# Convolution taps and the masked B C product read from PSUM, with a new order of the mixer step

## What is computed

```python
xn = rmsnorm(modulated layernorm of x)
z, xBC, dt = split(xn @ in_proj_w.T)                 # 1024, 1280 (1024 x + 128 B + 128 C), 16
pad = jnp.pad(xBC, ((0, 0), (DC - 1, 0), (0, 0)))    # DC = 4 taps, causal
conv = sum(pad[:, k:k + l, :] * conv_w[:, k] for k in range(DC)) + conv_b
xBC = conv * sigmoid(conv)
dt = softplus(dt + dt_bias)
# per chunk of 128 tokens, 16 heads of 64:
Y_diag = einsum('bcln,bcsn,bhcls,bcshp->bclhp', Cm, Bm, Lmat, X)   # (C B^T) masked, times exp(segment sums)
Y_off  = einsum('bcln,bchpn,bhcl->bclhp', Cm, states, exp(Acs))
y = (Y_diag + Y_off + D * xh) * (z * sigmoid(z))
y = rmsnorm(y); x1 = x + y @ out_proj_w.T
# then: layernorm, router (top 8 of 64 experts), experts, weighted sum
```

## Time and profile before

| | |
|---|---|
| median of 3 runs | 6409.54 us |
| the profiled execution | 6412.97 us |
| its span | 6411.1 us |
| PE busy over the span | 5781.9 us (90%) |
| DVE busy | 3957.1 us (62%) |
| ACT busy | 2733.7 us (43%) |
| POOL busy | 3763.9 us (59%) |
| mean granted PE clock | 0.951 |

### The profile page before, as it was taken

The page is one execution under the profiler, slowest core; times in us unless marked ns, Lnnn a source line. Parts: engine busy times, 40 slices in busy tenths (PEclk is TensorE's granted clock), DMA queues, the critical chain, the costliest instruction groups (busy, mean ns, idle before and its releaser), DMA issues. The chain is left out here.

```text
span 6411.1 us, 109995 instructions
## 1 busy us (share of the span) xinstructions
PE 5781.9 (90%) x28797; PEld 4345.1 (68%) x28798; DVE 3957.1 (62%) x10033; ACT 2733.7 (43%) x5780; POOL 3763.9 (59%) x2980
## 2 busy tenths in 40 slices
PE   2888888888888888888859999999999999999899
PEld 0556555565565565565548888888788888888787
DVE  1888888888888888888834444444344444444355
ACT  1555555555555555555513333333333333333322
POOL 0466666666666666666645555555555555555477
PEclk8899999999999999999979999999999999999999
DMA  9243343333343333333348887887877777887687
GB/s 351 107 124 119 106 131 120 111 130 107 117 136 105 119 125 105 122 122 105 129 123 194 196 217 173 213 196 175 228 155 176 186 164 179 211 214 196 106 269 256
DMA packets 338146, 1028.39 MB, mean 160 GB/s; under 512 B 55060, under 2 KB 59412, under 8 KB 337124
## 3 DMA queue, kind: packets, MB, share of 16 engines
q1 hardware_dynamic: 175512, 669.44, 30.3%
q0 software_dynamic: 145568, 321.56, 25.7%
q10 hardware_dynamic: 16816, 34.37, 1.4%
HBM read 580.45 MB, written 444.74 MB: 160 GB/s over the span
## 5 line engine op out<-in xcount | busy, mean ns | idle before, releaser
L1324 POOL DMA_INDIRECT acc_dram<-y_e,ids x576 | 907.9, 1576 | 1115.6 <-ACT y_e L1397 680.3
L1205 PE MATMUL bank<-w_hi,x_hi 128*128 (+1 forms) x2560 | 1058.0, 413 | 0.0
L1205 PE MATMUL bank<-w_hi,x_lo 128*128 (+1 forms) x2560 | 1002.3, 392 | 0.0
L1205 PE MATMUL bank<-w_lo,x_hi 128*128 (+1 forms) x2560 | 1001.5, 391 | 0.0
L938 DVE SCALAR_TENSOR_TENSOR acc<-raw,conv_w,acc 128x128 f32<-128x128 f32 x1920 | 820.3, 498 | 7.3 <-ACT acc L665 7.3
L602 POOL DMA_INDIRECT list_dram<-tok_id,pos x512 | 633.3, 1237 | 155.9 <-issue 154.6
L1415 DVE TENSOR_TENSOR h_lo<-bank,h_hi 128x256 fp32r<-128x256 f32 x576 | 243.5, 423 | 753.5 <-ACT h_hi L1386 746.8
L1397 ACT ACTIVATE y_e<-bank,xg_e 128x512 f32<-128x512 f32 x576 | 396.4, 688 | 693.4 <-PE bank L1205 649.1
L1316 POOL DMA_INDIRECT xg_e<-h_dram,ids x576 | 572.0, 993 | 195.0 <-issue 174.1
L1391 ACT ACTIVATE th_f<-bank 128x256 f32<-128x256 f32 x576 | 221.3, 384 | 1017.6 <-PE bank L1205 964.1
L770 PE MATMUL bank<-xn_t,w_in 128*128 128x128 f32 x5120 | 590.5, 277 | 66.4 <-ACT xn_t L644 66.4
(11 more groups left out here) (248 smaller groups left out, 10997.2 us busy)
## 6 DMA issues: line engine op xcount, KB each, us to landing
hi_dram<-w_hi_m SPq DMA_DIRECT2D x130, 768.0 KB, 7.4
lo_dram<-w_raw SPq DMA_DIRECT2D x130, 768.0 KB, 8.8
w_hi<-hi_dram SPq DMA_DIRECT2D x130, 768.0 KB
w_lo<-lo_dram SPq DMA_DIRECT2D x130, 768.0 KB
w_raw<-in_w_experts_dram SPq DMA_DIRECT2D x128, 768.0 KB
acc_dram<-zeros ACTq DMA_DIRECT2D x2, 16640.0 KB, 102.5
acc_c<-acc_dram SPq DMA_DIRECT2D x128, 256.0 KB, 3.5
h_dram<-h SPq DMA_DIRECT2D x64, 288.0 KB
```

What stands on the lines that cost most here:

```text
L1205: last = nc.tensor.matmul(acc, a, b, start=(i == 0), stop=(i == len(terms) - 1))
L1324: pool.indirect_dma_start(acc_dram[r % NACC], bass.IndirectOffsetOnAxis(ap=ids[:, r:r + 1], axis=0), y[:, r % YSLOTS, :], None, compute_op ...
```

## The change

Three things change in `mixer`.

1. **No copy of the projection.** The tile `raw` is gone. Instead `xn_t`, the normalised input, keeps the last 3 columns of the chunk before in front (`OLD` = 3), and each of the 40 matmuls of the projection has 131 columns instead of 128, so that PSUM holds all that the taps need. The projection comes in four groups of 3, 3, 3 and 1 blocks, in `half(1)`, `half(0)`, `half(6)` and `half(7)` (with dt). Taps 0 (ACT) and 1 to 3 (DVE) read them there. PSUM is held until the taps are done: yoff, which writes `bank[3]`, now waits for `taps`.
2. **The masked product stays in PSUM**, in `half(4)`, where DVE reads it for lm times it. The router's matmuls, which write the same bank, now wait for `m_done`.
3. **A new order** of the step. PE: the input projection, router, ydiag, states, yoff, z, y transposed, output projection, rank. ACT: exponentials of the rows before the normalisation of t; y copied before y is squared; the gate of z does not wait for y, since `gz` has two places. DVE: the carry comes first, the place of the token last, behind x1.

```diff
@@ mixer: tiles, groups @@
-        raw = sb("raw", [P, 2, NE, TAPS - 1 + P])
+        xn_t = sb("xn_t", [P, KD, TAPS - 1 + P])
+        XGROUPS = 4
+        OLD = TAPS - 1
-        gz = sb("gz", [P, DI])
+        gz = sb("gz", [P, 2, DI])
-        gm = sb("gm", [P, P])
+        def group(g):
+            return range(3 * g, min(3 * g + 3, NE))
+
+        def raw_of(i):
+            return half((1, 0, 6, 7)[i // 3])[:, i % 3 * (OLD + P):(i % 3 + 1) * (OLD + P)]
@@ ACT @@
-                        nc.scalar.copy(xn_t[:].rearrange("p k t -> p (k t)"), half(0)).then_inc(S["xnT_sb"], 1)
+                        act.wait_ge(S["carry"], f + 1)
+                        nc.scalar.copy(xn_t[:, :, OLD:], half(0).rearrange("p (k t) -> p k t", k=KD)).then_inc(S["xnT_sb"], 1)
+                    if c is not None:
+                        for j in range(2):
+                            act.wait_ge(S["rows_ps"], 2 * c + j + 1)
+                            nc.scalar.activation(lm[:, j * DI:(j + 1) * DI], (bank[3] if j == 0 else bank[1])[:], ACT.Exp).then_inc(S["l_exp"], 1)
                     if t is not None:
                         act.wait_ge(S["ln2_stat"], t + 1)
...
-                        nc.scalar.copy(raw[:, 1 - p, 4 * g:4 * g + n, TAPS - 1:],
-                                       half(1 - g % 2)[:, 0:n * P].rearrange("p (n t) -> p n t", n=n)).then_inc(S["raw_sb"], 1)
...
-                            last = nc.scalar.activation(acc[:, i, :], raw[:, 1 - p, i, 0:P], ACT.Identity,
+                            last = nc.scalar.activation(acc[:, i, :], raw_of(i)[:, 0:P], ACT.Identity,
@@ PE @@
-                                    last = nc.tensor.matmul(half(1 - g % 2)[:, i * P:(i + 1) * P], w_in[:, k, m:m + P],
+                                    last = nc.tensor.matmul(raw_of(i), w_in[:, k, m:m + P],
                                                             xn_t[:, k, :], start=(k == 0), stop=(k == KD - 1))
...
                         pe.wait_ge(S["h2T_sb"], t + 1)
+                        if c is not None:
+                            pe.wait_ge(S["m_done"], 2 * c + 2)
...
+                            pe.wait_ge(S["taps"], XGROUPS * (f + 1))
+                            pe.wait_ge(S["dt_raw"], f + 1)
+                        at_least(pe, S["state_done"], c)
+                        for j in range(2):
+                            last = nc.tensor.matmul(bank[3][:, j * 512:(j + 1) * 512], xbc[:, p, 9, :],
+                                                    state[:, j * 512:(j + 1) * 512], start=True, stop=True)
+                        last.then_inc(S["yoff_ps"], 1)
@@ DVE @@
+                    if f is not None:
+
+                        at_least(dve, S["z_ps"], 2 * f)
+                        ts(xn_t[:, :, 0:OLD], xn_t[:, :, P:P + OLD], col(starts, f), None, ALU.mult).then_inc(S["carry"], 1)
-                        tt(gm[:], half(4)[:, 0:P], tri[:], ALU.mult)
+                        tt(half(4)[:, 0:P], half(4)[:, 0:P], tri[:], ALU.mult)
-                               gm[:].unsqueeze(1).to_broadcast([P, 8, P]), ALU.mult).then_inc(S["m_done"], 1)
+                               half(4)[:, 0:P].unsqueeze(1).to_broadcast([P, 8, P]), ALU.mult).then_inc(S["m_done"], 1)
-                                        last = stt(out=acc[:, i, :], in0=raw[:, 1 - p, i, k:k + P], scalar=conv_w[:, i, k:k + 1],
+                                        last = stt(out=acc[:, i, :], in0=raw_of(i)[:, k:k + P], scalar=conv_w[:, i, k:k + 1],
                                                    in1=acc[:, i, :], op0=ALU.mult, op1=ALU.add)
```

More of the change, by code:

```diff
@@ L708, in step @@
                         nc.scalar.activation(xr[:], h[:], ACT.Copy, scale=rr[:]).then_inc(S["xr_done"], 1)
+                    if f is not None:
+                        act.wait_ge(S["z_ps"], 2 * f + 1)
+                        at_least(act, S["y_done"], f - 1)
+                        nc.scalar.activation(gz[:, 1 - p, 0:512], half(0), ACT.Tanh, scale=0.5).then_inc(S["z_th"], 1)
+                    if f is not None:
+                        act.wait_ge(S["z_ps"], 2 * f + 2)
+                        nc.scalar.activation(gz[:, 1 - p, 512:1024], half(1), ACT.Tanh, scale=0.5).then_inc(S["z_th"], 1)
+                    if c is not None:
+                        act.wait_ge(S["yT_ps"], c + 1)
+                        at_least(act, S["out_ps"], c)
+                        nc.scalar.copy(y_t[:].rearrange("p k t -> p (k t)"), bank[2][:]).then_inc(S["yT_sb"], 1)
                     if c is not None:
@@ L783, in step @@
                     if c is not None:
-                        pe.wait_ge(S["l_exp"], 2 * c + 1)
-                        at_least(pe, S["state_done"], c)
-                        for j in range(2):
-                            last = nc.tensor.matmul(bank[3][:, j * 512:(j + 1) * 512], xbc[:, p, 9, :],
-                                                    state[:, j * 512:(j + 1) * 512], start=True, stop=True)
-                        last.then_inc(S["yoff_ps"], 1)
                         pe.wait_ge(S["btok_sb"], c + 1)
@@ L799, in step @@
                         last.then_inc(S["rt_ps"], 1)
+                    if c is not None:
+                        pe.wait_ge(S["x1s_done"], c + 1)
+                        pe.wait_ge(S["m_done"], 2 * c + 2)
+                        for hh in range(NH):
+                            last = nc.tensor.matmul(bank[1][:, hh * HD:(hh + 1) * HD], lm[:, hh * P:(hh + 1) * P],
+                                                    x1s[:, hh * HD:(hh + 1) * HD], start=True, stop=True)
+                        last.then_inc(S["ydiag_ps"], 1)
                     if c is not None:
@@ L830, in step @@
                         last.then_inc(S["yT_ps"], 1)
+                    if c is not None:
+                        pe.wait_ge(S["yT_sb"], c + 1)
+                        pe.wait_ge(S["yoff_sb"], c + 1)
+                        for i in range(KI):
+                            last = nc.tensor.matmul(half(7), y_t[:, i, :], w_out[:, i, :], start=(i == 0), stop=(i == KI - 1))
+                        last.then_inc(S["out_ps"], 1)
                     if t is not None:
@@ L837, in step @@
                         nc.tensor.matmul(half(2)[:, EXPERTS:2 * EXPERTS], ones_bf[:], picked[:], start=True, stop=True).then_inc(S["rank_ps"], 1)
-                    if c is not None:
-                        pe.wait_ge(S["yT_sb"], c + 1)
-                        pe.wait_ge(S["yoff_sb"], c + 1)
-                        for i in range(KI):
-                            last = nc.tensor.matmul(half(7), y_t[:, i, :], w_out[:, i, :], start=(i == 0), stop=(i == KI - 1))
-                        last.then_inc(S["out_ps"], 1)
                 steps(pe, step)
@@ L1042, in step @@
                             dve.wait_ge(S["z_th"], 2 * f + j + 1)
[L1043 removed]
+                            stt(out=gz[:, 1 - p, j * 512:(j + 1) * 512], in0=gz[:, 1 - p, j * 512:(j + 1) * 512], scalar=1.0,
                                 in1=half(j), op0=ALU.add, op1=ALU.mult).then_inc(S["gz_done"], 1)
[L1045 to L1057 removed]
                     if ws is not None:
@@ L1076, in step @@
                         ts(ve2[:], mv2[:, 1:2], LN_EPS, None, ALU.add).then_inc(S["ln2_var"], 1)
+                    if t is not None:
+                        dve.wait_ge(S["rank_ps"], t + 1)
+                        place.mark(stt(out=key[:], in0=half(2)[:, 0:EXPERTS], scalar=-1.0, in1=nbase[:], op0=ALU.mult, op1=ALU.add))
+                        tt(nbase[:], nbase[:], half(2)[:, EXPERTS:2 * EXPERTS], ALU.subtract).then_inc(S["rank_done"], 1)
+                        at_least(dve, list_st[1 - p], 16 * TOPK * (t // 2))
+                        ts(tok_id[:, 1 - p:2 - p], tok_id[:, 1 - p:2 - p], 2.0 * P, None, ALU.add)
+                        place.wait()
+                        place.mark(tt(key[:], key[:], picked[:], ALU.mult))
+                        place.wait_apart(passed)
+                        place.mark(nc.vector.max(out=kmax[:], in_=key[:]))
+                        place.wait()
+                        place.end()
+                        ts(pos[:, 1 - p, :], kmax[:], -1.0, float(KEY), ALU.mult, ALU.add).then_inc(S["pos_done"], 1)
                 steps(dve, step)
```

112 lines of the change are left out of this document (32 added, 80 removed).

## The result

The changed kernel takes **6626.38 us** (median of 4 runs, 6621.94 to 6629.32), the kernel before 6408.94 in the same comparison (6404.81 to 6410.18). The ratio is 1.0339, 95% interval 1.0326 to 1.0352: slower by 3.4%. The forecast was 6350 us, with a range up to 6450: wrong in sign and outside the range.

A forecast was written before the change was run, and what follows sets the result against it. It took the loop of waits between DVE and PE ending a 47.79 us step as the bound. New loop 45.8 plus clock 1.0 gives 46.8 us, 61 us less over 62 steps: 6350 us, range 6285 to 6450.

The forecast's parts named there:

- Taps and products: DVE, reading PSUM: 30 taps fall from 12.85 to 7.5 us, two lm products to 2.4; 6.6 us less.
- The new loop without the clock: Mixer step counted from yoff to the next yoff along PE's work and waits: 45.8 us.
- the wait of 3.0 us for the rank: PE idle before the transposes of x until DVE's nbase releases rank_done: a new 3.0 us per step.
- I take 1.0, which is 1.5 us in two steps of three: PE's clock loss per step behind the new idle stretch, taken between bounds of nothing and 3.4 us.
- a wait of 1.3 us: PE before the router: ACT's last tap 0 and its copy of the router's input, with handoffs 1.3 us.
- Rival B: Slower: PE idles for the rank and its clock falls every step; 49.2 us a step, 6497 us; 17%.
- the forecast's 58%: Chance given to the forecast itself: 46.2 to 47.5 us a step, 6311 to 6392 us.
- the long form: PE's clock staying at 1.2 GHz for 6 to 7 us behind the rank's wait, costing 3.4 us.
- Rival C: No gain: DVE's taps and products stay slow, or clock and POOL losses eat 2.0 us; 12%.
- rival A: PE's clock stays up: 45.8 us a step, 124 us less in all, 6286 us; 13%.
- up to 0.8 us may come back here: POOL's list starts about 3 us later and the normalisation it feeds delays two ACT taps: up to 0.8 us.
- About 4 us of cover lie between taps and yoff: DVE's taps end near 42 us into the step, yoff starts at 45.8: about 4 us of slack.

The follow-up runs named there:

- Experiment 5: Changed kernel with the masked product back in SBUF (tile gm): 6704.29 us.
- experiment 3: Changed kernel with POOL's eight list DMAs ahead of r2: 6608.97 us; with the rank also moved to half(5): 6424.84 us.
- the rank's bank: Changed kernel with the rank in half(5) instead of half(2), so the transposes of x need not wait for its read: 6662.1 us alone.
- the kernel of 6372 us: The kernel of 6196 us with ACT's copy of the transposed input (xn_t) ahead of the exponentials and the copy of B: 6372.48 us.
- the kernel of 6260 us: The kernel of 6372 us with states between router and ydiag on PE: 6259.93 us.
- the kernel of 6196 us: Changed kernel with list DMAs early, rank in half(5), and the router's input transposed and copied before the last projection group: 6196.23 us.
- The best kernel: The kernel of 6372 us with ydiag ahead of the router on PE: 6015.48 us.
- experiment 6: Changed kernel with the rank again before the output projection and DVE's place work again ahead of x1: 6609.98 us.
- experiment 4: Changed kernel with the router's input transposed on PE and copied on ACT ahead of the last projection group's work: 6461.03 us.

## Why the prediction was wrong

**Taps and products: right.** 30 taps in 7.9 us, median 340 ns, two products in 2.35, as in the lower bound that I took. The shortest tap takes 339 ns from PSUM against 336 from SBUF, the median 340 against 339. The 120 against 58 cycles that the Trainium skill gives (VectorE: DVE Perf Modes, "The TRN2 errata") would be 65 ns more, by my estimate from its figures; the tap from PSUM does not show that. Experiment 5 bears out that the second SBUF tensor cost something, on both engines.

**The new loop without the clock: right, to 0.7 us.** The projection at full clock, x1 without a wait, y transposed plus ACT's copy, the wait of 3.0 us for the rank: each came as forecast. The forecast loop without clock losses was 45.8. The measured one is 41.44 + 3.1 (rank's wait) + 0.6 (router's wait) = 45.1.

**The clock: the step that failed.** "I take 1.0, which is 1.5 us in two steps of three" was too little in two ways. The term was mis-sized: the loss behind the rank's wait comes in 9 steps of 10 (the transposes take 1.06 us, the full clock, in 6 of 61) and costs 2.7 us in the step shown. And the sum had no term for the place before the router, where I had a wait of 1.3 us in plain numbers and asked only how long it was, not what stands around it. With yoff gone from there it costs 3.3 us of clock. 45.1 + 2.7 + 3.3 is 51.1, and the step takes 51.22.

**Rival B** had the right sign and the right first mechanism, at 49.2 us a step. It was short of the second fall, so 6497 instead of 6626. Its 17% and the forecast's 58% were the wrong way round: against it I held that the long form was needed each time, and it came nearly each time. Its own threshold, 2.0 us per step, is passed by either fall. Rival C fell, and so did rival A.

**POOL: "up to 0.8 us may come back here"** was mis-sized. With the late list the router waits 2.34 us or more in 5 of the 62 steps of the changed kernel, and mostly 4.7 once the rank's wait is gone; with the list early it waits under 1 us in every step. In the changed kernel itself it mostly hides behind the rank: taking it away gives 17 us (experiment 3), but together with the rank's bank 201.

**"About 4 us of cover lie between taps and yoff"** was right in that the taps no longer bound yoff: DVE's wait for yoff was forecast as 6 us and is 7.57 in the step shown.

## What to carry to other kernels

When a change makes PE the only bound, cost each wait on PE by what stands around it. The same wait before the router cost very different amounts of clock, besides the wait itself: 0.88 us cost some 3.3 in 52 steps of 56 with ydiag behind it, and nothing in 32 of 35 with states (512 columns) behind it; 2.34 us cost some 6.5 with ydiag behind it and 3.1 with states. So fill a wait with work that is already ready, even narrow work, before shortening it. When an edit that removes a wait gains nothing, look for the second limit on the same consumer before dropping the edit, since here one edit that alone lost 36 us and one that alone gained 17 gained 201 together. Shortening a wait in front of wide work can move it to narrow work and lose (6196 to 6372 us).

## What the runs showed of the hardware

The granted clock behind a wait depends on the work on both sides. All rows are views of stretches with the columns above. First the kernel of 6372 us (1.51 us of wait, then router and ydiag, 64 columns):

```profile
1519.10:1525.90 6.80, 6.80 (x34) 6.80 (x34) 1.60 (x8) 4.30 (x7) 6.15 (x6) 0.50 0.02 2
1525.90:1529.00 3.10, 3.10 (x6) 1.40 (x6) 0.00 (x0) 0.00 (x0) 2.19 (x4) 0.55 0.02 0
```

PE is busy for all of these 9.9 us, and still at 1.2 GHz until close to their end. The same wait with states (512 columns) right behind the router, in the kernel of 6260 us:

```profile
1517.50:1520.30 2.80, 2.79 (x5) 1.15 (x6) 1.39 (x7) 1.87 (x4) 2.80 (x2) 0.64 0.00 0
```

And a longer wait, 2.54 us, with the projection (131 columns) behind it, in the kernel of 6196 us:

```profile
1514.70:1516.50 1.80, 1.79 (x8) 1.79 (x9) 1.15 (x3) 1.80 (x3) 0.00 (x0) 0.50 1.01 416
1516.50:1518.50 2.00, 2.00 (x13) 2.00 (x13) 2.00 (x3) 0.70 (x1) 1.22 (x1) 0.63 1.02 427
1518.50:1520.50 2.00, 2.00 (x20) 2.00 (x19) 0.43 (x4) 1.16 (x3) 1.92 (x3) 1.00 0.36 151
```

The best kernel has a granted clock of 1.00 from 300 to 2700 us and a mean step of 41.5 us, with waits of 1.10, 0.68 and 0.31 in each. The mean steps of these three are 47.4, 45.7 and 44.4 us, and their waits 1.2, 1.6 and 1.5 more than its own, so they lose 4.7, 2.6 and 1.4 us of clock. A wait of 1.10 before the output projection (512 columns) cost no clock in any step, one of 2.40 none in 48 of 62 (experiment 6). So neither the wait nor the work behind it decides alone, and the same pair does not give the same clock in every step (4 of 56 in the changed kernel). What sets that apart is open. The Trainium skill (TensorE: Matmul & The Clock Gate, "What's actually happening") says that the clock follows how busy PE has been recently. The rows agree that recent activity counts. But the busy time that the profile prints for PE is full here while the clock falls in ydiag and stays down, so a full busy share in a profile does not show that the clock is up. Why narrow matmuls stand beside the losses was not tried, nor why in the early-transposes kernel of experiment 4 some stretches of steps pay behind the rank and others behind the router.

The other surprise is experiment 5: when DVE's product reads a second SBUF tensor while POOL works, both engines are slower, and it is POOL whose median moves (1277 to 1828 ns) while DVE's hardly does (1220 to 1225, mean 1217 to 1353). The kernel before shows both as well: taps of up to 1985 ns on DVE, and on POOL a product of 512 columns (L573; L579 in the changed kernel, where its median is 1272; which DVE instruction it met there was not looked at):

```profile
L573 POOL TENSOR_TENSOR h<-hn,mod x64: 1264/1901/1918, 146.7 to 3115.4; 128x512 f32<-128x512 f32 x64
```
